# Layer-norm scaling moved to GpSimd, SBUF tiles realigned, and the attention loop written in another order, in a fused adapter, attention and gated-MLP kernel

## What is computed

```python
# 1. conditional adapter with layer norm (weights picked by itok_B_0_8), 2. attention, residual
h = relu(x @ w1 + b1);  u = x + (h @ w2 + b2)
n = (u - mean(u)) * rsqrt(var(u) + 1e-5) * gamma + beta
q, k, v = n @ Wq.T (16 heads of 16), n @ Wk.T, n @ Wv.T (one key/value head)
x1 = x + softmax(causal(q k / 4)) v @ Wf.T + bf
# 3. conditional MLP (part of its second layer picked by itok_B_0_15): 256 -> 1024 -> 256
y = gelu(x1 @ fc1.T + b) @ [fc2 ; expert].T + b
# 4. gated ternary MLP: 256 -> 1024 -> 1024 -> 1024 -> 256, residual
g = silu(y W1 s1) * (y W2 s2);  g = gelu(g H1 t1);  g = gelu(g H2 t2)
out = x1 + (g W3) s3
```

## Time and profile before

| | |
|---|---|
| median of 3 runs | 1109.22 us (1109.03 to 1109.38) |
| profiled execution | 1108.92 us, span 1107.1 us |
| PE busy | 1084.2 us, 98% of the span |
| DVE busy | 808.7 us, 73% |
| ACT busy | 597.2 us, 54% |
| POOL busy | 174.8 us, 16% |
| passes 1 to 13 of stage one | 18.9 us each |
| a tile of stage two, a pair of stage three | 22.2 us, 146.4 us |

### The profile page before, as it was taken

How to read it: one execution, slowest core, us unless ns; L and a number is a source line. 1 busy time by engine, 2 the same in 40 slices (tenths; PEclk the granted TensorE clock), 3 DMA queues, 4 the chain that set the end, 5 groups by cost and what they waited for, 6 DMA issues and landing times.

```text
span 1107.1 us, 18530 instructions
## 1 busy us (share of the span) xinstructions
PE 1084.2 (98%) x6155; PEld 864.0 (78%) x6155; DVE 808.7 (73%) x1416; ACT 597.2 (54%) x1004; POOL 174.8 (16%) x192
## 2 busy tenths in 40 slices
PE   7899999999989999999999999999999999999998
PEld 4567777777757888888888888888888888888886
DVE  4888787878887676555687765888748787577875
ACT  2456666666655445433566555655637555455643
POOL 2122232222364434520000000000000000000000
PEclk9899999999999999999999999999999999999999
DMA  6445656567675565646054431344422444304421
GB/s 170 76 89 120 119 127 111 129 116 185 128 266 179 181 207 199 220 143 209 20 171 148 155 117 57 131 136 159 143 76 66 154 160 150 114 18 141 145 95 39
DMA packets 82256, 148.59 MB, mean 134 GB/s; under 512 B 15504, under 2 KB 42016, under 8 KB 82080
## 3 DMA queue, kind: packets, MB, share of 16 engines
q1 hardware_dynamic: 68946, 123.51, 37.4%
q10 hardware_dynamic: 13262, 24.52, 8.2%
HBM read 107.63 MB, written 30.41 MB: 125 GB/s over the span
## 4 chain that ended last, share of the span: by engine, by line
PE 94%; DVE 3%; ACT 1%; issue 1%; DMA 0%; POOL 0%; SPq 0%; DVEq 0%; ACTq 0%; POOLq 0%
PE bank L1813 37%; PE bank L1775 11%; PE bank L1530 7%; PE bank L1825 5%; PE bank L1442 5%; PE bank L1751 4%; PE bank L1745 4%; PE bank L1461 3%; PE bank L1445 3%; PE bank L1480 3%; PE bank L1378 2%; PE bank L1366 1%; PE bank L1401 1%; PE bank L1518 1%; PE bank L1500 1%; PE bank L1482 1%
## 5 line engine op out<-in xcount | busy, mean ns | idle before, releaser
L1813 PE MATMUL bank<-op_hi,w_ring 128*128 128x512 f32 x896 | 348.6, 389 | 0.0
L1813 PE MATMUL bank<-op_lo,w_ring 128*128 128x512 f32 x896 | 348.6, 389 | 0.0
L1259 DVE TENSOR_TENSOR op_lo<-x_blk,op_hi 128x512 fp32r<-128x512 f32 x288 | 193.7, 684 | 30.4 <-ACT op_hi L878 30.3
L878 ACT ACTIVATE op_hi<-x_blk 128x512 fp32r<-128x512 f32 x288 | 162.8, 620 | 73.5 <-PE bank L1813 69.3
L1813 PEld LDWEIGHTS bank<-op_lo,w_ring 128*128 128x128 f32 x896 | 168.2, 188 | 35.0
L1813 PEld LDWEIGHTS bank<-op_hi,w_ring 128*128 128x128 f32 x896 | 168.1, 188 | 35.0
L1028 DVE TENSOR_REDUCE neg_max<-bank 128x2 f32<-128x512 f32 (+1 forms) x192 | 125.1, 686 | 6.6 <-PE bank L1445 3.6
L679 ACT ACTIVATE p<-bank 128x512 f32<-128x512 f32 x192 | 107.1, 592 | 33.8 <-PE bank L1461 30.6
L902 ACT ACTIVATE x_blk<-x_blk,scales 128x512 f32<-128x512 f32 x96 | 69.3, 722 | 67.0 <-DVE x_blk L1312 28.9
L1775 PE MATMUL bank<-tile_hi,ffn_w 128*128 128x512 f32 x256 | 101.6, 397 | 0.0
L1775 PE MATMUL bank<-tile_lo,ffn_w 128*128 128x512 f32 x256 | 100.9, 394 | 0.0
(11 more groups left out here) (148 smaller groups left out, 1784.5 us busy)
## 6 DMA issues: line engine op xcount, KB each, us to landing
w_ring<-hid_scratch SPq DMA_DIRECT2D x112, 512.0 KB, 4.6
hid_scratch<-comb ACTq DMA_DIRECT2D x8, 1792.0 KB, 8.0
q_t<-q_high SPq DMA_DIRECT2D x64, 128.0 KB, 4.1
comb<-in_hid_d ACTq DMA_DIRECT2D x6, 768.0 KB, 4.7
xt<-in_x_t SPq DMA_DIRECT2D x16, 256.0 KB, 3.6
xtok<-in_x_tok SPq DMA_DIRECT2D x16, 256.0 KB
resid<-in_x_t SPq DMA_DIRECT2D x16, 256.0 KB, 3.1
x_scratch<-x SPq DMA_DIRECT2D x16, 256.0 KB, 2.6
```

The lines of the kernel that those rows point to most:

```text
L878: nc.scalar.activation(op_hi[:, o % OP_RING, k], x_blk[:, operand_home(o), k], ACT.Copy).then_inc(s["op_hi"], 1)
L1259: nc.vector.tensor_tensor(op_lo[:, o % OP_RING, k], x_blk[:, operand_home(o), k], op_hi[:, o % OP_RING, k].bitcast(F32), ALU.subtract).the ...
L1813: last = mm(banks[first_bank + m][:, :], w, read(v[:, q % OP_RING, k, :]), start=k == 0 and v is op_hi and i not in (P2, P3), stop=k == KB ...
```

## The change

It has three parts. (1) `normalise` goes from DVE to POOL, where it stands right behind `rstd_of`; DVE waits for it before it writes `u` anew. (2) Two tiles that nothing reads, `line_pad` (448 bytes) and `second_pad` (64 bytes), are put in, and `two_pad` is taken out. (3) In passes with softmax and tail, the order on PE, ACT and SP is written anew, and in the last pass `first_tile(0)` and `first_tile(1)` go between and behind the two halves of `products`. Passes -1 and 0 keep their order on PE and ACT.

Start of tiles modulo 512, before and after (the others that matmuls read keep theirs, between 64 and 480):

| tile | before | after |
|---|---|---|
| `ffn_w` | 128 | 64 |
| `g_parts0`, `g_parts1` | 96 | 64 |
| `y` | 96 | 64 |
| `tile_hi`, `tile_lo`, `w_ring`, `fc1_hi`, `fc1_lo`, `fc2a_*`, `fc2b_*`, `x_blk`, `op_hi`, `op_lo` | 64 | 64 |

```diff
-TWO_PAD = 1
...
+        sb("line_pad", [P, 112])
         ffn_w = sb("ffn_w", [P, FFN_COLS], F32R)
...
+        sb("second_pad", [P, 16])
 
         xa = yc = sb("tile_in", [P, KD, TW])
...
-        two_pad = sb("two_pad", [P, TWO_PAD], F32, two)
...
 # SP
                 move_high(b + 2, (slot + 2) % SLOTS)
+                load_resid(b)
                 move_maxima(b + 1, (slot + 1) % SLOTS)
                 store_x1(b - 1)
-                load_resid(b)
...
 # POOL
+            def normalise(n):
+                pool.wait_ge(s["rstd_ready"], n + 1)
+                settle(pool, "pool_settled")
+                for t in range(NT):
+                    nc.gpsimd.tensor_scalar(norm[:, t, :], u[:, t, :], moments[:, t, 0:1], rstd[:, t:t + 1],
+                                            ALU.subtract, ALU.mult).then_inc(s["norm_ready"], 1)
...
                 if front:
                     rstd_of(b + 2)
+                    normalise(b + 2)
...
 # ACT: exponential(b, 4) behind affine, norm_parts, attention_out; then
+                    exponential(b, 4)
                     exponential(b, 5)
                     exponential(b, 6)
-                if tail:
-                    attention_out(b - 1)
                 if front:
                     queries_high(b + 2)
                 if softmax:
                     exponential(b, 7)
+                    exponential(b, 8)
                 if front:
                     keys_copied(b + 2)
+                    move_low(b + 2, (slot + 2) % SLOTS)
                 if softmax:
-                    exponential(b, 8)
                     exponential(b, 9)
-                if front:
-                    move_low(b + 2, (slot + 2) % SLOTS)
-                    keys_high(b + 2, (slot + 2) % SLOTS)
+                    exponential(b, 10)
                 if maxima:
                     maxima_out(b + 1)
+                if front:
+                    keys_high(b + 2, (slot + 2) % SLOTS)
                 if softmax:
-                    exponential(b, 10)
                     exponential(b, 11)
...
 # DVE: the two instructions of normalise are gone from every pass
+                if not is_first(n):
+                    dve.wait_ge(s["norm_ready"], NT * n)
```

More of the change, by code:

```diff
@@ L601, in _ @@
             rstd_of(0)
+            normalise(0)
             pool.wait_ge(s["const_loaded"], 80)
@@ L741, in iteration @@
                     exponential(b, 3)
-                    exponential(b, 4)
                 if front:
@@ L969, in add_adapted @@
                 nc.vector.tensor_scalar(veps[:, :], moments[:, :, 1], EPS, None, ALU.add).then_inc(s["veps_ready"], 1)
-            def normalise(n):
-                dve.wait_ge(s["rstd_ready"], n + 1)
-                for t in range(NT):
-                    nc.vector.tensor_scalar(norm[:, t, :], u[:, t, :], moments[:, t, 0:1], rstd[:, t:t + 1],
-                                            ALU.subtract, ALU.mult).then_inc(s["norm_ready"], 1)
             def norm_rest(n):
@@ L1065, in iteration @@
                     add_adapted(b + 2)
-                    normalise(b + 2)
                     split_fc1(0)
@@ L1189, in _ @@
             add_adapted(0)
-            normalise(0)
             split_queries_weights()
@@ L1639, in iteration @@
                     max_scores(b + 1, ahead, 1)
+                if tail:
+                    products_transposed(b - 1, 0, front)
                 if softmax:
@@ L1670, in iteration @@
                     max_scores(b + 1, ahead, 6)
+                if softmax:
+                    scores(b, slot, 5)
+                if maxima:
                     max_scores(b + 1, ahead, 7)
@@ L1673, in iteration @@
                     project_queries(b + 2, tail)
+                if softmax:
+                    scores(b, slot, 6)
                 if maxima:
@@ L1684, in iteration @@
                     max_scores(b + 1, ahead, 10)
+                    max_scores(b + 1, ahead, 11)
                 if softmax:
                     scores(b, slot, 9)
-                if maxima:
-                    max_scores(b + 1, ahead, 11)
                 if tail:
                     project_out(b - 1, front)
+                if softmax:
+                    scores(b, slot, 10)
                 if front:
                     values_transposed(b + 2)
-                if softmax:
-                    scores(b, slot, 10)
-                    scores(b, slot, 11)
                 if maxima:
                     maxima_transposed(b + 1)
+                if softmax:
+                    scores(b, slot, 11)
             pe.wait_ge(s["warm_made"], 1)
```

29 lines of the change are left out of this document (11 added, 18 removed).

## The result

The changed kernel takes 1115.2 us, the median of 5 runs (1113.8 to 1117.75), against 1109.22 before (1108.72 to 1109.81 over 5 runs): ratio 1.0058, 95% interval 1.0044 to 1.0072. It is slower; the prediction said 1101.0 and faster. The profiled execution took 1113.8 us, its span is 1112.0; it is the shortest of the five, whose mean granted clocks go from 0.995 (this one) down to 0.990 (the 1117.75), so the profile shows 4.9 of the 6.0 us between the medians.

What follows compares the result with a forecast made beforehand. PE bounds the kernel (busy 98% of the span), so only its own work or waits count. Terms -6.2 - 2.1 + 0.2 + 0.4 - 0.5 = -8.2 us from 1108.92 give 1100.7, stated as median 1101.0; range 1097.5 to 1105.5.

Steps and rivals of the forecast that it cites:

- the price of `normalise` on POOL: Each 128x256 instruction on POOL was taken at 0.40 us, from the line through the mask's rows.
- the other end: Upper price for one `normalise` instruction on POOL: 1.56 us, the dearest form there, with two tensor inputs of 512.
- the point at which it decides: About 0.95 us an instruction on POOL, where the cover ahead of `norm_transposed` is gone.
- Slower: Rival: POOL needs as much as for its two-input form, `norm` comes late in 13 passes; about 1123 us; chance 0.05.
- The start: Prologue and pass -1, where nothing hides `normalise`: +0.2 us, or +4.8 at 1.56 an instruction.
- The loop: Thirteen passes in the new order with `normalise` on POOL: -0.16 us a pass, -2.1 in all.
- The new order wins nothing: Rival: the tight copy and exponentials eat the 0.16 us a pass; 1103.1 us; chance 0.13.
- The starts: Stages two and three: equal starts modulo 512 speed up matmuls; -5.0 us and -1.2 us, -6.2 together.
- The 256 columns: Stage two's 48 matmuls of 256 columns: taken at no change, bounds nothing and 2.3 us less in all.
- The pads do nothing: Rival: 233 ns a matmul has another cause than the starts, so only -2.0 is left; 1107.2 us; chance 0.10.
- Pass 14 and 15: Pass 14: longer mask wait, +0.4 us; pass 15: mask wait filled by `first_tile(0)`, -0.5, between -1.5 and +0.5.
- The clock: Rival: start's half-clock stretch, costing 3.3 us, goes (1097.7) or another like it comes (1104.4); chance 0.06 each.

Runs made afterwards that it cites:

- e5: Kernel before plus 56 unneeded GpSimd instructions in stage three, eight times seven forms on a scratch tile; 1109.4 us, run once.
- e2: Changed kernel with `normalise` back on DVE, new starts and new order kept; 1104.23 us, ratio 0.9962 to the kernel before.
- e4: Kernel before with the new starts alone, plus the 256-column weights (`fc2b_hi`, `fc2b_lo`) at 96 modulo 512; 1103.31 us, ratio 0.9946.
- e7: As e6, with `norm_transposed` behind `max_scores` 4 and 5 on PE in passes 1 to 13; 1106.95 us, ratio 0.9985.
- e1: Kernel before with the change of the tiles' starts alone, order and `normalise` as before; 1102.0 us, ratio 0.9940.
- e6: Changed kernel with `normalise` on DVE in the prologue and passes -1 and 0, on GpSimd from pass 1; 1107.76 us, ratio 1.0000.
- e10: As e2, with ACT's `attention_out` behind exponential 5 in the last pass; 1102.01 us, ratio 0.9948.
- e3: Kernel before with `normalise` on GpSimd alone, starts and order as before; 1118.77 us, ratio 1.0091.
- e8: Kernel with the new starts alone, but `ffn_w` at 320 modulo 512; 1101.67 us, run once.
- e11: Kernel before with `two_pad` out, `ffn_w` at 192 and `w_ring` at 96 modulo 512, streamed tiles at 64; 1119.42 us, run once.
- e12: Kernel before with `two_pad` out, `op_hi` and `op_lo` at 128 modulo 512, `ffn_w` still at 128; 1114.83 us, run once.
- e15: Kernel before with e4's starts and PE's new last-pass order; loop order, ACT's lists and `normalise` as before; 1101.48 us, ratio 0.9932.
- e14: Changed kernel with 10 more idle-time matmuls in the prologue and 16 more in pass -1; 1113.61 us, ratio 1.0036.

## Why the prediction was wrong

**The step that failed** is the price of `normalise` on POOL: "I take 0.40, since the mask too reads one tensor". It is 1.235, nearer the other end (1.56) and above the point at which it decides (0.95), so `norm_transposed` waits, which the prediction said it would not. The number of tensor inputs is not what sets the price: with one input each, the mask costs 0.9 ns a column, a copy of 256 columns 0.40 us, and `tensor_scalar` 3.3 ns a column (e5). From the price the rival *Slower* followed, to which I gave 0.05; the mask's line was no argument for so small a chance, since the operation itself had no row in the trace. The Trainium skill (GPSIMD Engine Reference, Engine selection) says that one input is "roughly line-rate"; for this form the trace does not agree: two instructions take 2.47 us on GpSimd and 0.73 on DVE, 3.4 times as much.

**The start**: priced 0.2, at the other end 4.8; measured 4.4. The waits for `norm` there are 6.5 us in place of 1.9. With 1.235 the same sum gives 3.5 (2 x 2.47 less 2 x 0.73). The other 0.9 is not separated from the clock: in pass -1, which holds the stretch at half clock, the changed kernel takes 22.6 us; with `normalise` on DVE that pass takes 21.3 to 21.4 where it holds such a stretch (e2, e4, e7) and 19.7 to 20.1 where it doesn't (before, e1, e6, e10). Pass 0 was not in my list, since the loop's cover was assumed for it: it loses 1.7 us to GpSimd (e3 against e1), hidden in the comparison because the kernel before lost 1.6 to its clock at the same place.

**The loop**: -2.1 was priced, +3.7 came. Two errors. The first is GpSimd's price. The way from price to wait was about right: at 1.235 the rival's own sum gives 2 x (1.235 - 0.95) = 0.57 a pass, and `norm_transposed` waits 0.48; only its 16 us were too dark, at a price of 1.56 and without the waits for DVE's maxima (0.24 a pass in e2's chain, 0.01 to 0.02 in the changed kernel's), which go where PE waits for `norm`. The second: the order wins nothing without GpSimd either (e2). I cut the wait of `max_scores` 7 but did not follow DVE's list to units 5 and 6, which now come early for it. So two rivals came true at once, *Slower* (0.05) and *The new order wins nothing* (0.13).

**The starts**: -5.0 in stage three was right to a tenth, and so was -0.15 a tile for the 24 matmuls. The 256 columns, taken at 0 with bounds of 0 and -2.3, lost 0.09 a tile: the sign was outside my bounds. -6.2 became -5.6. The rule behind it was too narrow (modulo 512); for 512 columns it holds modulo 256 (e8, e11, e12). The rival *The pads do nothing* is out (e1). It rested on the Trainium skill (SBUF — State Buffer, Who interferes with whom), by which PE's two read ports are independent. The traces do not agree with what the prediction drew from that: 226.7 against 233.3 ns by the starts of the two operands alone.

**Pass 14 and 15**: +0.4 and -0.5; e2 against e1 gives 0.0 for both together. The sum was right by luck. The two waits for the mask moved as forecast: pass 14's went from 0.97 to 1.19 (+0.2), pass 15's 1.24 is gone. But scores 6 of pass 15 now wait 1.18 for exponential 4, since ACT's copy stands ahead of it, which I did not see: the order of pass 15 wins 1.3 (e15) and ACT's list costs 1.3 (e10). In the changed kernel a stretch at half clock lies on top of it, 2.3 us (68.16 against e2's 65.86).

**The clock**: its stretches move with every change and between executions. One of 6.83 us is worth 1.6 (pass 0, e1) to 2.3 us (behind the loop, e2) here, not 3.3.

## What to carry to other kernels

An operation that no row shows on its new engine has no price until it is run: a neighbour with as many inputs is no bound, and the point from which it decides belongs in the chances. Moving work off an engine that waits anyway helps only if the chain through that work has slack, and the slack must be counted to its last reader (here norm, affine, rounding, projection). When an order is written anew, follow each other engine's list one or two units beyond the wait that was removed, in the passes at the end too.

## What the hardware showed

- fp32 matmuls of 512 columns: 226.7 to 227.0 ns where weights and streamed operand start at the same byte modulo 256, 232.4 to 233.4 where they don't (eight pairs of starts). Of 256 columns it is the other way round in the two pairs that were tried: 119.8 with both at 64, 117.9 and 118.3 with one of the two at 96.
- `tensor_scalar` on GpSimd with two operations and two scalars in SBUF: 0.37 us and 3.3 ns a column, 1.23 us for 256, against 0.40 us for a copy of 256; up to 2.59 us for 256 beside DVE instructions with two inputs in SBUF.
- A stretch of 6.83 us at half clock cost 1.6 and 2.3 us, less than half its length; in pass 0 PE idled 1.3 us less meanwhile (e1). A wait of 1.2 us in pass 15 was followed by such a stretch in five of six profiles. With PE kept busy through the waits of the start, the stretch stood in pass 0 in place of pass -1 (e14); whether the one caused the other is not shown, since stretches in the start also come and go between executions of the same code.
